# A decoder layer in which each batch's cross-attention is put beside the next batch's self-attention

## The reference

```
x = x + self_attention(layernorm(x))      # 16 query heads, 4 key/value groups, width 128, causal
x = x + cross_attention(layernorm(x), ctx)# 32 query heads, 8 key/value heads, width 16, no mask
x = x + ffn(layernorm(x))                 # 8 experts, the best 2 for each token, and a shared expert
```

## Time and profile before

| | us |
|---|---|
| median of 3 runs | 2100.18 (2099.85 to 2102.96) |
| profiled execution, its own time | 2103.39 |
| profiled execution, its span | 2101.7 |
| PE busy | 1958.1 |
| DVE busy | 1117.3 |
| ACT busy | 967.1 |
| POOL busy | 298.6 |

### The profile page before, as it was taken

The page is one execution under the profiler, slowest core; times in us unless marked ns, Lnnn a source line. Parts: engine busy times, 40 slices in busy tenths (PEclk is TensorE's granted clock), DMA queues, the critical chain, the costliest instruction groups (busy, mean ns, idle before and its releaser), DMA issues.

```text
span 2101.7 us, 30693 instructions
## 1 busy us (share of the span) xinstructions
PE 1958.1 (93%) x10847; PEld 1457.1 (69%) x10847; DVE 1117.3 (53%) x2250; ACT 967.1 (46%) x1778; POOL 298.6 (14%) x763
## 2 busy tenths in 40 slices
PE   6899989998999999988999989998899699999999
PEld 4677756775777667655555555555498699999998
DVE  7333433343334343455777777778544365555564
ACT  3444433343334343334676666765522255555421
POOL 1000000000000000041233322322003211111142
PEclk9999999999999999989999999999888799999999
DMA  3000000001000000000000160000003367776553
GB/s 130 31 1 1 21 32 1 1 21 32 1 1 1 21 1 1 5 7 1 1 6 2 41 239 1 1 1 1 28 16 133 127 232 241 247 238 243 203 149 118
DMA packets 74129, 135.17 MB, mean 64 GB/s; under 512 B 3952, under 2 KB 33648, under 8 KB 73968
## 3 DMA queue, kind: packets, MB, share of 16 engines
q1 hardware_dynamic: 68848, 116.29, 16.3%
q0 software_dynamic: 5120, 16.78, 2.4%
HBM read 96.35 MB, written 36.70 MB: 63 GB/s over the span
## 4 chain that ended last, share of the span: by engine, by line
PE 83%; DVE 11%; issue 3%; ACT 3%; DMA 0%; DVEq 0%; POOL 0%; ACTq 0%
PE ps L141 44%; PE ps L147 9%; PE ps L914 7%; PE ps L993 6%; PE ps L835 6%; PE ps L1016 4%; PE ps L1005 4%; DVE xmax L1444 3%; DVE nmax L1420 1%; DVE stats L154 1%; DVE xo L1521 1%; DVE probs L1428 1%; DVE al L1473 1%; ACT ah L1239 1%; ACT probs L1196 1%
## 5 line engine op out<-in xcount | busy, mean ns | idle before, releaser
L1444 DVE TENSOR_REDUCE xmax<-ps 128x1 f32<-128x512 f32 x512 | 347.0, 690 | 120.8 <-PE ps L993 118.0
L1263 ACT ACTIVATE xp<-ps 128x1024 f32<-128x1024 f32 x256 | 263.6, 1031 | 157.3 <-PE ps L1005 156.5
L1196 ACT ACTIVATE probs<-ps,nmax 128x128 f32<-128x128 f32 (+3 forms) x256 | 135.2, 528 | 312.9 <-DVE nmax L1420 312.1
L1420 DVE TENSOR_REDUCE nmax<-ps 128x1 f32<-128x128 f32 (+3 forms) x256 | 124.9, 488 | 231.9 <-PE ps L835 226.3
L993 PE MATMUL ps<-k,q 128*128 128x512 f32 x496 | 220.3, 444 | 25.4 <-DVE xmax L1444 21.3
L835 PE MATMUL ps<-k_t,q_t 128*128 128x128 f32 (+3 forms) x512 | 201.6, 477 | 0.0
L993 PEld LDWEIGHTS ps<-k,q 128*128 128x128 f32 x496 | 93.6, 189 | 149.0 <-DVE xmax L1444 94.2
L914 PE MATMUL ps<-pt,v_s 128*128 128x128 f32 (+3 forms) x512 | 158.9, 455 | 24.4 <-ACT v_s L1245 20.9
L147 PE MATMUL ps<-ident,probs 128*128 128x128 f32 x704 | 126.9, 285 | 44.0 <-DVE probs L1428 29.1
L1005 PE MATMUL ps<-q3m,k 128*128 128x512 f32 x512 | 161.9, 398 | 0.0
L147 PEld LDWEIGHTS ps<-ident,probs 128*128 128x128 f32 x704 | 90.4, 146 | 99.9 <-issue 67.6
(11 more groups left out here) (187 smaller groups left out, 3678.3 us busy)
## 6 DMA issues: line engine op xcount, KB each, us to landing
w_raw<-in_w_t SPq DMA_DIRECT2D x54, 704.0 KB
w_raw<-in_w_t SPq DMA_DIRECT2D x27, 768.0 KB
rows_x<-w_raw SPq DMA_DIRECT2D x1, 11776.0 KB, 37.6
mixed<-rows_x SPq DMA_DIRECT2D x23, 512.0 KB, 5.6
rows_y<-y_s SPq DMA_DIRECT2D x23, 512.0 KB, 2.8
w_raw<-in_w_qkv_t SPq DMA_DIRECT2D x4, 1536.0 KB, 6.8
res<-in_x SPq DMA_DIRECT2D x4, 1024.0 KB, 12.3
w_raw<-in_w_proj_t SPq DMA_DIRECT2D x4, 1024.0 KB, 5.6
```

The lines of the kernel that those rows point to most:

```text
L1196: act.activation(probs[:, u % 4, 0:w], ps[:, S_BANK + u % 2, 0:w], ACT.Exp, bias=nmax[:, u % 4:u % 4 + 1], accum_out=rsum[:, u % 4:u % 4 + ...
L1263: act.activation(xp[:, kv % 2, h, 2 * pair:2 * pair + 2, :], ps[:, XST + 2 * pair:XST + 2 * pair + 2, :], ACT.Exp, scale=X_SCALE).then_inc ...
L1420: dve.tensor_reduce(nmax[:, u % 4:u % 4 + 1], ps[:, S_BANK + u % 2, 0:w], AX_X, ALU.max, negate=True).then_inc(s_max, 1)
L1444: dve.tensor_reduce(xmax[:, slot, i, h:h + 1], ps[:, bank + u % 2, :], AX_X, ALU.max, negate=True).then_inc(s_xmax, 1)
```

## The change

The two attention stages become one list, `step_plan`, with 351 steps. Batches are outermost now: 16 pairs (batch, group) in this order, one unit for each of the first 256 steps. Each engine walks the whole list, without loops. Chains are cut in halves of 6 matmuls, and the 20 halves of a pair (batch, group) are spread over 16 steps. An item of cross-attention takes its maxima in 8 steps, two matmuls in each (`most`), and 5 steps after the last of them its transposed scores in 8 steps, also two in each (`alike`); a new item starts every 8 steps, the first one at step 80.

```diff
+def max_step(m):
+    return UNITS * (GROUPS + 1) + KV * m
...
+def exp_step(m):
+    return max_step(m) + 13
...
+N_STEP = exp_step(ITEMS - 1) + 10
...
+        parts = [("out", g - 1, t, half) for t in range(TOK_TILES) for half in range(HALVES)]
+        parts += [("in", g + 1, n, half) for n in range(len(PIECES)) for half in range(HALVES)]
...
+            step = UNITS * g + 2 + p * UNITS // len(parts)
...
+        for r in range(KV):
+            at(s + r, "a", "most", m, r, 0)
+            at(s + r, "b", "most", m, r, 1)
+            at(e + r, "a", "alike", m, r, 1)
+            at(e + r, "b", "alike", m, r, 0)
+        for j in range(TOK_TILES):
+            at(e + 2 * j + 2, "xpv", "xpv", m, j)
+        at(s + 8, "end", "split_most", m)
+        at(s + 9, "end", "turn_most", m)
+        at(e + 9, "end", "turn_out", m)
...
+    for step in steps:
+        head, tail = step["part"][:1], step["part"][1:]
+        low = sorted(step["b"], key=lambda op: op[0] == "most")
+        ops += (step["first"] + step["a"] + step["pv"] + step["turn"] + head + low + step["xpv"] + step["end"] + tail)
```

All of it must fit in 8 PSUM banks at once, so scores, turns, chains, heads' results, maxima and cross results have one bank each, and the transposed scores two (one pair):

```diff
-        S_BANK, T_BANK, O_BANK, G_BANK = 0, 2, 4, 6
-        XST, XS, XO, XT = 0, 4, 6, 7
+        S_BANK, T_BANK, G_BANK, O_BANK, XS, XST, XO = 0, 1, 2, 3, 4, 5, 7
```

```diff
+                elif op[0] == "reload" and op[1] == "in":
+                    g = op[2]
+                    chain_done(sp, "in", g - 1, len(PIECES) - 1)
...
+                    for part, w in enumerate((wh, wl)):
+                        sp.dma_start(w[:, :, :].bitcast(F32), w_parts[g % GROUPS, 0:len(PIECES), part]
+                                     .rearrange("n p c -> p n c")).then_inc(s_again_in, 16)
...
+                elif op[0] == "turn_most":
+                    m = op[1]
+                    sp.wait_ge(s_mc, m + 1)
+                    sp.dma_start(max_parts[m % 2], mx_t[0:2 * XG * TOK_TILES, :]).then_inc(s_mo, 16)
+                    sp.wait_ge(s_mo, 16 * m + 16)
```

Each head's strip has 48 rows (50 with the maxima), at partition 0 or at partition 64, and the matmul reads only these rows. In the list a matmul of one half stands next to one of the other half: `alike` in the upper rows and `most` in the lower ones, later in the step the other way round. A matmul of maxima waits for the maximum of the one before it, a pair of transposed scores for the last exponential:

```diff
+                    if n:
+                        pe.wait_ge(s_xmax, n)
+                    pe.matmul(ps[:, XS, :], q3[head_rows(h), m % KEPT, h // 2, i * P:(i + 1) * P],
+                              k3[head_rows(h), m % KEPT, :], start=True, stop=True).then_inc(s_xs, 1)
...
+                    if n and hf == 1:
+                        pe.wait_ge(s_xe, n)
+                    ins = pe.matmul(ps[:, XST + hf, :], k3[head_rows_max(h), m % KEPT, j * P:(j + 1) * P],
+                                    q3[head_rows_max(h), m % KEPT, h // 2, :], start=True, stop=True)
```

More of the change, by code:

```diff
@@ L37, in mark @@
         self.n += 1
-        return self.start + self.n
+        return self.n
     def seal(self, eng, ins):
         eng.wait_ge(self.sem, self.mark(ins))
[L47 to L57, removed]
@@ L62 @@
[L62 to L90, removed]
@@ L94 @@
[L94 to L135, removed]
@@ L138, in products @@
-def products(pe, dst, pairs):
+def products(pe, dst, pairs, first=True, last=True):
     for n, (lhs, rhs) in enumerate(pairs):
-        last = pe.matmul(dst, lhs, rhs, start=(n == 0), stop=(n == len(pairs) - 1))
-    return last
+        ins = pe.matmul(dst, lhs, rhs, start=(first and n == 0), stop=(last and n == len(pairs) - 1),
+                        skip_group_check=not (first and last))
+    return ins
 def turned(pe, dst, src, ident):
     return pe.matmul(dst, src, ident, start=True, stop=True, is_transpose=True)
+KV, XG, XD = 8, 4, 16
@@ new lines, with in_order @@
+PLAN = step_plan()
+def in_order(*kinds):
+    return [op for op in PLAN if op[0] in kinds]
+CHAINS = [("in", 0, 0), ("in", 0, 1)] + [op[1:4] for op in in_order("part") if op[4] == HALVES - 1]
+TURNS = in_order("turn", "values", "turn_row", "turn_ctx", "turn_most", "turn_out")
+ROW_OPS = [(1, 0, t) for t in range(TOK_TILES)] + [op[1:] for op in in_order("row")]
+STAGED = [op for op in TURNS if op[0] == "turn_ctx" or op[:2] == ("turn_row", 2)]
+SPREADS = [0] + [op[1] for op in in_order("spread")]
@@ new lines, in give @@
+            def give(dst, g, t, half):
+                if half == 0 and t == 0:
+                    pe.wait_ge(s_al, QPG * g + QPG)
+                    if g < GROUPS:
+                        pe.wait_ge(s_wl, SPLITS.index(("out", g, QPG - 1)) + 1)
+                    else:
+                        pe.wait_ge(s_again_out, 32 * (g - GROUPS + 1))
+                toks = slice(t * P, (t + 1) * P)
+                pairs = [(a[:, (QPG * g + h) % (QPG + 1), toks], w[:, h, :])
+                         for a, w in ((ah, woh), (ah, wol), (al, woh)) for h in range(QPG)]
+                return products(pe, dst, pairs[half * N_PART:(half + 1) * N_PART], half == 0, half == HALVES - 1)
```

1204 lines of the change are left out of this document (588 added, 616 removed).

## The result

The changed kernel takes **2188.58 us** (median of 4 runs, 2187.49 to 2190.71), beside 2100.01 us (2099.59 to 2102.96) for the kernel before in the same session: ratio 1.042, 95% interval 1.040 to 1.044. It is 4.2% slower. The forecast was 2066 us with a range of 1945 to 2160: wrong in sign and outside the range.

The account below looks back on a forecast made before the run. PE was taken to bound both attention stages. Start 26.5, self-attention alone 274.4, both 885, cross-attention alone 252 plus 8, drain 25, feed-forward 589.1 plus 8 gave 2068 us of span, rounded to 2066 after corrections; range 1945 to 2160.

Parts of the forecast that it names:

- A third of the way gives 3.15 us: Cross-attention alone, last 80 steps: between 2.77 us a step and 3.9 at half clock; 252 us, plus 8 for output chains.
- the circle through one bank: Cross-attention alone: maxima matmul, maximum and back through the single bank take 1.27 us, twice a step; matmuls 0.2 to 0.3 longer at half clock.
- The drain: End of attention: last maxima through POOL, PE, ACT and DMAs, then 8 pairs and the end, 25 us.
- The end runs at half clock throughout: Rival for the last 80 steps: 0.75 us more each, 60 us in all, 2126 us; chance 0.09.
- Steps 0 to 79: Self-attention alone: 3.43 us a step, with 0.11 for single banks, 274.4 us in all.
- Transfers: Reloads, strips and maxima by DMA: issued some steps ahead, they cost nothing unless SP's queue is held.
- the rival: Stored parts come late because SP's queue holds reloads behind two DMAs of maxima: 84 us, 2150 us; chance 0.04.
- 162 x 5.16 - 16: Steps with both stages: 5.16 us each, 176 of them 908 us; the last pair's missing projection halves take 16 off.
- the change of shape costs: Steps with both stages: each visit from 128 rows to 64 and back costs 0.31 us, two a step.
- the pair overlaps: Steps with both stages: two short matmuls in different array halves run side by side, 0.46 us a step instead of 0.92.
- queues in order: Rival: pairs wait for ACT's exponential at single banks, 0.5 us a step, 88 us, 2154 us; chance 0.15.
- the feed-forward: Stage after attention: 589.1 us plus 8 for a late third weight, there about 27 us into the stage.

Follow-up runs that it names:

- full_rows: Changed kernel with all maxima and transposed-score matmuls reading 128 rows, leaving out what keeps two heads apart (a time probe): ratio 1.0065 to the kernel before.
- rows128_tail: Changed kernel with zero-padded 128-row query strips, three in turn, read in full only from item 23 on, 48 or 50 rows before: ratio 1.026 to the kernel before.
- warm: Changed kernel plus unused 128-row matmuls from item 23, three behind each maxima matmul, one where narrow products follow: ratio 1.025 to the kernel before.
- warm48: Changed kernel plus unused matmuls from item 23, three or one behind each maxima matmul, reading 48 rows instead of 128: ratio 1.057 to the kernel before.
- two: Changed kernel with a second PSUM bank for maxima from item 23, the scores' bank: ratio 0.995 to the kernel before.
- banks: Changed kernel with a second maxima bank from item 23 and a second pair of banks for transposed scores from item 24: ratio 0.990 to the kernel before.
- best2: Changed kernel with second banks for scores and chains up to step 77, for maxima from item 23, for transposed scores from item 24: ratio 0.983, 2050.64 us.
- warm_two: Changed kernel with a second maxima bank from item 23 and one unused matmul behind each maxima matmul that no narrow product follows: ratio 1.035 to the kernel before.
- start: Changed kernel with second banks for scores and chains up to step 77, where cross-attention's are free: ratio 1.036 to the kernel before.
- rows128: Changed kernel with all items' matmuls reading 128 rows from query strips zero outside a head's rows, three strips in turn: ratio 1.0065 to the kernel before.

## Why the prediction was wrong

**The step that failed** is the price of the last 80 steps: "A third of the way gives 3.15 us". The upper end of that sum was good: half clock was forecast at 3.9 us a step and is 3.80, and the circle through one bank grew by the 0.3 us that was allowed. What was wrong was the place between the ends: the clock of this stretch was read from the start of the kernel before, by how much PE is busy (0.83 with 9.58 of 14 us), a stretch of 128-row matmuls. Here it was 0.50 with PE busy for 44 of 50 us. (Such shares don't compare across clocks: a slow matmul counts as busy for longer, 0.79 us in place of 0.49.) 80 steps at 3.80 in place of 3.15 are 52 of this stretch's 62 us, and 7.2 of the other 10 are a wait for loads. The whole miss of the sum is 121 us. The drain (12 us) ran at the same half clock; what that cost was not measured apart. "The end runs at half clock throughout" stood among the rivals with 0.09; by itself it gave 2126, since the rest of the sum was low too.

What the reading missed, as far as the runs show it, are the matmuls of 48 and 50 rows. With unused matmuls of 128 rows the clock was 1.00, with the same ones of 48 rows 0.50; with the kernel's own work in 128 rows it was 0.93 at 37 of 50 us busy, and full_rows' tail, at 0.88, is 50 us shorter; in rows128_tail it rose once the last 50-row matmul was over.

The Trainium skill (TensorE: Matmul & The Clock Gate, Part 1) says that the gate opens and closes by how busy PE has been recently. warm, beside the changed kernel, agrees with that; warm48, busy for 50.00 of 50 us at 0.50, does not, and the measurement decides. Nor are rows a switch: *two*, *banks* and *best2* kept 48 and 50 rows and had 0.72, 0.79 and 0.81 in their tails, and *warm_two*, with some 128-row fillers on top of *two*, had 0.61. What sets the level in such mixed stretches stays open.

**Steps 0 to 79** (+36): 7.8 us are the first item's loads, 11.5 the single banks (8 were allowed for), 4 the splits. The other 20 or so are not settled; *start* shows 11 us of waits for the turn's copy in them, which may have come in place of those removed. 16 steps took 57.8 to 61.5 us here for the 55 forecast.

**Transfers** were priced at nothing "unless SP's queue is held". It was: 25.2 us in four waits, by the stores ahead of each batch's first item, not by the reloads of weights of which the rival spoke. In the middle they are most of the difference: from 398.3 to 1231.7 us, 162 steps, it is 833 us, where the forecast's terms give 162 x 5.16 - 16 = 820, and two of these waits are 10.2 us.

**Right:** the change of shape costs (0.26 us a visit for 0.31), though no row showed it for rows; the pair overlaps (0.38 us a step for 0.46); queues in order don't decide (PE waits for the exponential 18.2 us in all); 16 middle steps take 81.0 to 83.5 us for 82 (88 to 89 where they hold a wait for a batch's first item); and the feed-forward is 3 us shorter than forecast. There the copy of the third weight stands 15 us into the stage, not 27; in ACT's timeline of the changed kernel this line answers to the earlier trace rows:

```profile
1610.54 1.48 ACT L1286 CAST w3h<-w_raw 128x1536 fp32r<-128x1536 f32 x1 [3.49 <-DMA w_raw<-in_w_t]
```

The Trainium skill (TensorEngine Tiling (Array Packing), Key Properties) says that a change of tiling mode drains the engine. The runs agree that it costs something for rows as for columns, by the 0.26 us above.

## What to carry over

- A stretch of short-contraction matmuls can lose TensorE's clock while the engine looks 87 to 100% busy, as the last 80 steps and warm48 did. Read the granted clock together with the rows that the matmuls use; where there is a form with zeros in the other rows, try it: here it also saved the changes of shape, which cost more than the overlap brought (93 us for 67.5).
- When banks run short in a merged schedule, share them only in the steps that need all: second banks at the two ends took this one from 1.042 to 0.983, nearly 6%, where the whole change had been forecast to bring 1.6%.
- Don't take a clock for a stretch from another stretch by busy share alone; price it at both levels, and give the low one a real chance.

## What the hardware showed that was not expected

- Two row tiles of 48 and 50 rows start within 0.01 us of each other and take 0.49 us each; going there from 128 rows and back costs 0.26 us.
- 128-row against 48-row unused matmuls, all else equal: granted clock 1.00 and 0.50 in the same 50 us, ratio 1.025 and 1.057. Without unused matmuls, 48 and 50 rows had anything from 0.50 to 0.88 in such a window (changed kernel, best2).
- Rows of zeros did as much for the clock as data: 0.91 over the tail of rows128, 0.88 over that of full_rows.
- Adding work to PE's queue made the kernel faster: ratio 1.042 without it, 1.025 with it (warm).
